# A selective scan whose C rows come by broadcast transfers, with two decay slots in PSUM and seven of 32 drives on GpSimd

## The reference

```python
sel = jnp.einsum('ble,se->bls', xc, sel_w)
dt_in = sel[..., :R_]
Bm = sel[..., R_:R_ + N_]
Cm = sel[..., R_ + N_:]
dt = jax.nn.softplus(jnp.einsum('blr,er->ble', dt_in, dt_w) + dt_b)
dA = jnp.exp(dt[..., None] * A)
dBu = dt[..., None] * Bm[:, :, None, :] * xc[..., None]

def step(h, inp):
    dA_t, dBu_t, C_t = inp
    h = dA_t * h + dBu_t
    y = jnp.einsum('ben,bn->be', h, C_t)
    return (h, y)
```

## Time and profile before

| what | value |
|---|---|
| median of 3 runs | 1655.74 us (1651.43 to 1656.33) |
| the profiled execution | 1655.36 us |
| its span in the trace | 1653.6 us |
| scan stage of the second pair, first scan to last gate product | 489.35 to 616.70 us |
| busy in the whole span | PE 85%, DVE 65%, ACT 42%, POOL 25% |

### The profile page before, as it was taken

The page is one execution under the profiler, slowest core; times in us unless marked ns, Lnnn a source line. Parts: engine busy times, 40 slices in busy tenths (PEclk is TensorE's granted clock), DMA queues, the critical chain, the costliest instruction groups (busy, mean ns, idle before and its releaser), DMA issues. The chain is left out here.

```text
span 1653.6 us, 16757 instructions
## 1 busy us (share of the span) xinstructions
PE 1409.3 (85%) x5750; PEld 572.7 (35%) x5770; DVE 1080.9 (65%) x1253; ACT 691.3 (42%) x979; POOL 415.6 (25%) x242
## 2 busy tenths in 40 slices
PE   6877879988987787998997778799999777789997
PEld 2222223246422222324632223232563222223265
DVE  3599825675559983567465997256746699635673
ACT  0455433234345553324425555332441655433244
POOL 3166600012006650002101764000210276300030
PEclk9989969998999996999898999699989899979998
DMA  8100020000000002000000000100000000010000
GB/s 253 58 0 1 1 64 1 1 1 1 13 0 0 1 1 64 1 1 1 1 13 0 0 1 20 45 1 1 1 1 13 0 0 1 23 29 1 1 1 13
DMA packets 24693, 26.02 MB, mean 16 GB/s; under 512 B 4611, under 2 KB 21795, under 8 KB 24099
## 3 DMA queue, kind: packets, MB, share of 16 engines
q1 hardware_dynamic: 24002, 20.61, 4.3%
q10 hardware_dynamic: 608, 4.34, 0.9%
HBM read 20.73 MB, written 4.21 MB: 15 GB/s over the span
## 5 line engine op out<-in xcount | busy, mean ns | idle before, releaser
L401 POOL TENSOR_TENSOR scratch<-scratch 128x1024 f32<-128x1024 f32 x124 | 306.2, 2470 | 468.4 <-ACT scratch L865 314.6
L1074 DVE TENSOR_TENSOR_SCAN scratch<-ps,scratch 128x1024 f32<-128x1024 f32 x128 | 292.2, 2283 | 5.5 <-ACT ps L858 5.5
L547 PE MATMUL ps<-scratch,consts 128*128 128x512 f32 x512 | 253.4, 617 | 14.0 <-ACT work L889 12.0
L412 POOL TENSOR_TENSOR work<-work,rmax 128x512 f32<-128x512 f32 x64 | 67.5, 1054 | 695.3 <-DVE rmax L1224 695.3
L858 ACT ACTIVATE ps<-steps,vec 128x1024 f32<-128x1024 f32 x128 | 143.1, 1118 | 183.5 <-DVE scratch L1074 183.5
L592 PE MATMUL ps<-h_odd,w 64*128 64x512 f32 x512 | 175.1, 764 | 43.4 <-ACT scratch L898 43.4
L1126 DVE TENSOR_TENSOR scratch<-scratch,ps 128x1024 f32<-128x1024 f32 x108 | 131.8, 1221 | 118.8 <-PE ps L603 113.4
L898 ACT ACTIVATE scratch<-ps 128x1024 f32<-128x1024 f32 x108 | 110.6, 1024 | 228.7 <-PE ps L592 228.7
L1066 DVE TENSOR_TENSOR scratch<-steps,ps 128x1024 f32<-128x1024 f32 x128 | 156.1, 1220 | 23.2 <-PE ps L521 15.0
L521 PE MATMUL ps<-bc,pick 128*128 128x512 bf16 x244 | 78.7, 402 | 98.8 <-DVE scratch L1066 97.4
L603 PE MATMUL ps<-scratch,w 64*128 64x512 f32 x512 | 136.8, 609 | 10.3 <-DVE scratch L1126 10.0
(11 more groups left out here) (194 smaller groups left out, 1663.5 us busy)
## 6 DMA issues: line engine op xcount, KB each, us to landing
steps<-routed_table SPq DMA_DIRECT2D x128, 64.5 KB, 1.9
decayT<-in_decayT SPq DMA_DIRECT2D x8, 512.0 KB, 17.3
work<-in_table ACTq DMA_DIRECT2D x1, 2064.0 KB, 13.7
routed_table<-work SPq DMA_DIRECT2D x1, 2064.0 KB, 6.4
w<-in_w ACTq DMA_DIRECT2D x4, 512.0 KB, 21.1
out<-h_even SPq DMA_DIRECT2D x4, 512.0 KB, 2.6
bc<-in_x_next SPq DMA_DIRECT2D x3, 512.0 KB, 3.5
bc<-in_x_first SPq DMA_DIRECT2D x1, 512.0 KB, 3.8
```

Of the source, the lines that this page charges most:

```text
L401: pool.tensor_tensor(hc_slot(k), hs_slot(k), c_slot(k), ALU.mult).then_inc(sem["hc_ready"], 1)
L547: m = mm(ps[:, 6 + c, :], ident, hc_slot(k)[:, c * CH:(c + 1) * CH], start=(n == 0), stop=(n == NS - 1))
L1074: dve.tensor_tensor_scan(hs_slot(k), banks(DA_BANK), dbu_slot(k), 0.0, ALU.mult, ALU.add).then_inc(sem["scanned"], 1)
```

## The change

C no longer passes through PE and ACT. The C part of `sel` (16 rows of 1024 values per sequence) is copied from PSUM to SBUF (`c_rows`: by DVE for the first sequence, by ACT for the second), stored to memory by SP, and loaded back row by row, each time broadcast to all 128 partitions, into a ring of four slots. `spread_c` and `copy_c` are gone. The banks that held C become a second decay slot, so decay k waits for scan k-2. For seven states (5, 9, ..., 29) ACT copies the spread B to SBUF (`copy_b`) and POOL does the drive there in place (below: a POOL drive); their spreads stand one place earlier in PE's list. The last state's product is done by DVE in place of POOL.

```diff
+POOL_DRIVES = (5, 9, 13, 17, 21, 25, 29)
+B_ORDER = list(range(2 * NS))
+for _j in POOL_DRIVES:
+    B_ORDER[_j - 1:_j + 1] = [_j, _j - 1]
+C_RING = 4
...
-        DA_BANK = 2
+        def dA_bank(k):
+            return 2 + 2 * (k % 2)
...
             def move(pair, more):
+                sp.wait_ge(sem["c_rows"], at(pair, "c_rows", 1))
+                sp.dma_start(c_dram[0], c_rows(0)[NS:2 * NS]).then_inc(sem["c_stored"], 16)
+                sp.wait_ge(sem["c_stored"], at(pair, "c_stored", 16))
+                for k in range(2 * NS):
+                    g, n = divmod(k, NS)
+                    if k == 2:
+                        sp.wait_ge(sem["dt_ready"], at(pair, "dt_ready", 1))
+                    if k == C_RING:
+                        sp.wait_ge(sem["c_rows"], at(pair, "c_rows", 2))
+                        sp.dma_start(c_dram[1], c_rows(1)[NS:2 * NS]).then_inc(sem["c_stored"], 16)
+                    if k == NS:
+                        sp.wait_ge(sem["c_stored"], at(pair, "c_stored", 32))
+                    if k >= C_RING:
+                        sp.wait_ge(sem["hc_ready"], at(pair, "hc_ready", k - C_RING + 1))
+                    sp.dma_start(c_slot(k), c_dram[g, n].partition_broadcast(P))\
+                      .then_inc(sem[f"c_loaded{k % C_RING}"], 16)
...
+                    pool.wait_ge(*c_landed(pair, k))
+                    if k >= 3:
+                        pool.wait_ge(sem["y_summed"], at(pair, "y_summed", k - 2))
+                    pool.tensor_tensor(hc_slot(k), hs_slot(k), c_slot(k), ALU.mult).then_inc(sem["hc_ready"], 1)
+                    if k + 4 in POOL_DRIVES:
...
+                        pool.wait_ge(sem["b_copied"], at(pair, "b_copied", n_))
+                        pool.tensor_tensor(b_sb, u[:, j // NS, :], b_sb, ALU.mult).then_inc(sem["dbu_pool"], 1)
...
-                def spread_b(k):
+                def spread_b(i):
+                    k = B_ORDER[i]
...
-                    if k:
-                        pe.wait_ge(sem["dbu_ready"], at(pair, "dbu_ready", k))
+                    if i:
+                        last = B_ORDER[i - 1]
+                        if last in POOL_DRIVES:
+                            pe.wait_ge(sem["b_copied"], at(pair, "b_copied", POOL_DRIVES.index(last) + 1))
+                        else:
+                            pe.wait_ge(sem["dbu_ready"], at(pair, "dbu_ready", drives_up_to(last)))
...
                 def decay(k):
-                    if k:
-                        act.wait_ge(sem["scanned"], at(pair, "scanned", k))
+                    if k >= 2:
+                        act.wait_ge(sem["scanned"], at(pair, "scanned", k - 1))
+                    else:
+                        act.wait_ge(sem["dt_read"], at(pair, "dt_read", k + 1))
...
+                def copy_b(j):
+                    act.wait_ge(sem["b_ps"], at(pair, "b_ps", B_ORDER.index(j) + 1))
...
+                    act.activation(b_sb, banks(0), ACT.Copy).then_inc(sem["b_copied"], 1)
...
+                    if k + 2 in POOL_DRIVES:
+                        copy_b(k + 2)
...
                 def drive(k):
-                    dve.wait_ge(sem["b_ps"], at(pair, "b_ps", k + 1))
+                    if k in POOL_DRIVES:
+                        return
+                    dve.wait_ge(sem["b_ps"], at(pair, "b_ps", B_ORDER.index(k) + 1))
...
+                for c in range(NC):
+                    cols = slice(c * CH, (c + 1) * CH)
+                    dve.tensor_tensor(hc_slot(last)[:, cols], hs_slot(last)[:, cols], c_slot(last)[:, cols],
+                                      ALU.mult).then_inc(sem["hc_last"], 1)
```

More of the change, by code:

```diff
@@ L223, in build_tower, with drives_up_to, c_landed, c_rows @@
         kb = scratch[:, 0:8].rearrange("p a (w h k) -> p (a w) h k", w=2, h=H)
-        DA_BANK = 2
+        def dA_bank(k):
+            return 2 + 2 * (k % 2)
+        b_sb = work[:, 3 * T:4 * T]
+        def drives_up_to(k):
+            return k + 1 - sum(j <= k for j in POOL_DRIVES)
         def dbu_slot(k):
-            return scratch[:, 2 + k % 2]
+            return b_sb if k in POOL_DRIVES else scratch[:, 2 + drives_up_to(k) % 2]
         def c_slot(k):
-            return scratch[:, 4 + k % 2]
+            return scratch[:, (0, 1, 4, 5)[k % C_RING]]
+        def c_landed(pair, k):
+            return sem[f"c_loaded{k % C_RING}"], at(pair, f"c_loaded{k % C_RING}", 16 * (k // C_RING + 1))
+        def c_rows(g):
+            return (work[0:32, 0:T] if g else work[0:32, 3 * T:4 * T])
         def hs_slot(k):
@@ L384, in _ @@
             for pair in range(PAIRS):
[L386 to L406, removed]
+                for k in range(2 * NS - 1):
+                    if k in U_LATE:
+                        c = U_LATE.index(k)
+                        cols = slice(c * NCH, (c + 1) * NCH)
+                        pool.wait_ge(sem["dt_late"], at(pair, "dt_late", c + 1))
+                        pool.tensor_tensor(u[:, 1, cols], dt[:, 1, cols], xc[:, 1, cols],
+                                           ALU.mult).then_inc(sem["u_late"], 1)
+                    pool.wait_ge(sem["scanned"], at(pair, "scanned", k + 1))
+                    pool.wait_ge(*c_landed(pair, k))
[3 more added lines that the diff above has]
+                    if k + 4 in POOL_DRIVES:
+                        j = k + 4
+                        pool.wait_ge(sem["u_ready"], at(pair, "u_ready", 1))
+                        if j >= NS:
+                            pool.wait_ge(sem["u_late"], at(pair, "u_late", NN))
+                        n_ = POOL_DRIVES.index(j) + 1
+                        pool.wait_ge(sem["b_copied"], at(pair, "b_copied", n_))
+                        pool.tensor_tensor(b_sb, u[:, j // NS, :], b_sb, ALU.mult).then_inc(sem["dbu_pool"], 1)
@@ L523, in spread_b @@
                     m.then_inc(sem["b_ps"], 1)
[L525 to L528, removed]
-                    if k:
[L530 to L534, removed]
                 def sum_states(k):
                     g, n = divmod(k, NS)
-                    pe.wait_ge(sem["hc_ready"], at(pair, "hc_ready", k + 1))
+                    if k < 2 * NS - 1:
+                        pe.wait_ge(sem["hc_ready"], at(pair, "hc_ready", k + 1))
                     if n == 0:
                         pe.wait_ge(sem["sel_read"], at(pair, "sel_read", 2))
+                        pe.wait_ge(sem["c_rows"], at(pair, "c_rows", 2))
                         if g:
@@ L873, in _ @@
                 first_parts(1)
+                decay(0)
                 dt_above(1)
                 dt_size(1)
-                decay(0)
-                copy_c(0)
+                act.activation(c_rows(1), banks(SEL_BANK[1])[0:32], ACT.Copy).then_inc(sem["c_rows"], 1)
                 decay(1)
-                copy_c(1)
                 for k in range(2, 2 * NS):
```

40 lines of the change are left out of this document (25 added, 15 removed).

## The result

The changed kernel takes 1679.09 us in the median of four runs (1674.79 to 1687.07), the kernel before 1656.03 beside it: a ratio of 1.0151, with a 95% interval of 1.0108 to 1.0194. It is slower, by 23 to 25 us where 15 were forecast, and inside the range. The profiled execution has a span of 1678.6 us.

The account below looks back on a forecast made before the run. DVE sets the scan stage's pace. Clock falls cost 9.1 us a pair, gains give 5.3: 3.8 longer, 15 us over four pairs, from 1655.4 to 1670 us; the 8 in 10 range is 1637 to 1688 us.

Parts of the forecast that it names:

- the saved drives: Scan stage: seven drives a pair leave DVE, 7 x 1.14 = 8.0 us, but the saving goes into the stall.
- drive j-1: DVE's drive one state before POOL drive j; forecast to start at 4.93 instead of 3.62 us after scan j-4.
- The stall: DVE waits 1.31 us a round because PE's list has the sum of j-4 ahead of the spread of j-1.
- The gap: PE has nothing for 3.15 us each round ahead of the sum of j-3, while POOL does drive j and hc j-3.
- The clock's price: After the gap TensorE's clock halves and the spread of j+1 comes late: 1.3 us a round, 9.1 us a pair.
- The small DVE operations: Five a pair, 0.40 to 0.73 us each, hidden in the stall: together some 2.6, gain 2.0 us a pair.
- scans j-4 and j-3: DVE's scans four and three states before POOL drive j; small operations behind them were to fall into the stall.
- the copy's stall: Between the two sequences DVE waits 2.58 us as PE waits for the copy of y; forecast to go.
- Copy of y, first scan, end of stage: Three waits in the scan stage forecast to go or shrink, gaining 2.58, 0.19 and 0.57 us a pair.
- Clock holds, 1634: Rival: the clock holds in PE's gaps, the 5.3 us a pair gain remains, 1634 us; chance 0.20.
- The broadcasts: Rival: C row loads slower than 3.5 us a row (149 GB/s) can't keep up, near 1800 us; chance 0.07.
- The slow streams: Cited for the broadcast rival: 128 partitions at alike addresses ran at 103 GB/s; a row would take 5.1 us.

Follow-up runs that it names:

- filled_gap: The changed kernel with nine zero-weight matmuls behind the spread of j-1, in PE's gap ahead of the sum of j-3: 1654.9 us, 0.9954 of the kernel before.
- no_drives: The changed kernel with no drives on POOL, C rows still broadcast and the decay still in two slots: 1638.4 us, 0.9880 of the kernel before.
- product_first_filled2: The changed kernel with POOL's product hc of j-3 ahead of drive j, and six zero-weight matmuls ahead of the sum of j-2: 1644.4 us, 0.9932 of before.
- both_orders: The changed kernel with PE's spread of j-1 ahead of the sum of j-4 and POOL's product ahead of its drive: 1650.5 us, 0.9962 of before.

## Why the prediction was right, and which of its terms were not

- **Direction and mechanism.** Right, with one cost left out: the saved drives were eaten by a stall at drive j-1 and by a falling clock, and by small operations that stood. That the clock decides was half right. With the gap filled the kernel is no slower than before (0.9954), but neither is it with POOL's product first (0.9974), where the clock falls and the small operations hardly stand.
- **The stall.** 1.31 us forecast, 1.32 measured beyond the usual step (556.88, and again at 571.80). PE's list makes it: with the spread moved ahead of the sum it shrank to 0.27.
- **The gap.** 3.15 us forecast, 3.10 measured. POOL is what PE waits for, 115.0 us in the page.
- **The clock's price.** Mis-sized: 9.1 us a pair forecast, 4.7 measured in the profiled execution of filled_gap. The clock fell in most rounds, but not in all: the gap of 3.83 us at the sum of 546.07 left it alone. And part of the price was hidden under operations that stood anyway.
- **The small DVE operations.** This is the step that failed: "small DVE operations behind scans j-4 and j-3 fall into it", a gain of 2.0 us a pair. (The five take 2.9 us in the trace of before, where it had 2.6.) Behind scan j-3 POOL is inside its drive, and they stand until it ends; the three lines took 7.0 us a pair more (45.7 - 17.6 over four). The earlier trace rows showed only POOL being held, and in the kernel before none of these lines was ever long (means of 0.40, 0.73 and 0.67). The Trainium skill (SBUF — State Buffer, Who interferes with whom) has the rule: a DVE operation with both inputs in SBUF contends with GpSimd's reads, and "Issue order, not op shape, decides who blocks". The traces agree in both orders: POOL's 2.36 became 2.85 where DVE was first, DVE's 0.40 became 2.45 where POOL was. The change turned the order around.
- **The two errors met.** The drives' waits grew by 28.9 us where the stall and the clock less the copy's stall had been put at 62.8 ((1.31 + 1.3) x 7 - 2.58, four pairs); the small operations by 28.1 where 8.0 less was forecast. The one was 33.9 too high and the other 36.1 too low, so that the time came out as near as it did is in part luck. But not all: they stood in the stall's place, so each covers part of the other: taking away one alone gave 1.6 us (small operations), 6.2 (the list) or 18.9 (the clock) in the stages, and POOL's order, which takes most of the standing and part of the gap, 24.0; all three together, with POOL's order, 50.3.
- **Copy of y, first scan, end of stage.** Right: no_drives gains 3.4 us a pair by them, forecast 3.34. In the changed kernel PE waited 3.1 us for the copy in all four pairs, where the earlier trace rows have 12.0.
- **The rivals.** Clock holds, 1634: filled_gap made that case and came to 1655, with the small operations standing; with most of them free too, product_first_filled2 came to 1644. The broadcasts: 3.6 us a row, 146 GB/s by 512 KB, no wait. The slow streams that the prediction cited from the Trainium skill (DMA: Bandwidth & Descriptors, Latency and other measured facts) are those of rows 4 or 8 MiB apart. Here all partitions read one row, and at 3.6 us none of that shows.

What stays open: why the rest of the span differs by up to 9 us between kernels that are alike there, why the runs of filled_gap lie so far apart, and what decides whether a given gap drops the clock.

## What to carry to other kernels

Moving work to an engine that is not full costs more than its time: it changes who starts first at a shared resource, what stands behind it in other engines' lists, and how long TensorE is without work, so look at each list around the moved operation before counting the saving. Small DVE operations on two SBUF inputs belong, in this kernel, directly behind the event that also releases POOL, not inside its long operations; POOL then pays (2.85 us in place of 2.36). And when costs cover each other, removing one of them says little about its size: read the waits and the busy times together, and take all of them away once.

## What the runs showed of the hardware

The length of a gap alone did not tell whether the granted clock fell. Two sums, the first of the changed kernel, the second of both_orders, each behind a wait for POOL, and the granted clock while it ran:

```profile
546.07 1.98 PE L583 MATMUL ps<-scratch,consts 128*128 128x512 f32 x4 [3.83 <-POOL scratch L437]
546.07:548.05 1.98, 1.98 (x5) 0.87 (x6) 1.81 (x1) 0.92 (x2) 1.98 (x2) 1.00 0.49 165
```

```profile
566.14 3.64 PE L583 MATMUL ps<-scratch,consts 128*128 128x512 f32 x4 [2.16 <-POOL scratch L437]
566.14:569.50 3.36, 3.36 (x4) 1.32 (x5) 3.36 (x3) 0.76 (x1) 2.70 (x1) 0.50 0.48 156
```

Behind 3.83 us the sum ran at 2.4 GHz (1.98 us), behind 2.16 us at 1.2 GHz (3.64). With zero matmuls in the gap it was at 1.00 from 510 to 616 in the second pair (filled_gap).

DVE's operations with one input in PSUM kept their time beside a busy POOL: a drive took 1.21 to 1.22 us and a scan 2.26 to 2.29 wherever they stand by themselves in the traces before and after.
